# A post-norm decoder layer: the attention's weights loaded and split in smaller pieces

## The chip, the cores and the metric

The kernel runs on one core of one Trainium2 chip. The metric is the device time of one execution in microseconds (us). TensorE (PE) does the matrix products, ScalarE (ACT), VectorE (DVE) and GpSimd (POOL) the elementwise work, SyncE (SP) issues most of the transfers. ACT issues some transfers too. Each engine runs its own instructions strictly in the order written and meets the others by semaphores.

## The reference, cut to what matters

```python
# x: (8, 256, 256) f32; ctx: (8, 120, 256); Wq, Wk, Wv: (256, 1024); Wo: (1024, 256)
x = layernorm(x + attn(x, Wq, Wk, Wv, Wo, bo))     # 16 heads of 64, causal
x = layernorm(x + xattn(x, ctx, ...))              # 3 rounds of slot attention with a GRU
x = layernorm(x + ffn(x, gate, shared MLP, 8 experts, the best 2 per token))

def attn(x, Wq, Wk, Wv, Wo, bo):
    q, k, v = (x @ W, as 16 heads of 64) for Wq, Wk, Wv
    p = softmax(q k^T / 8 + causal mask)
    return (p v, heads joined) @ Wo + bo
```

## The kernel before, in words

The program has three stages, one for each line of the reference, with a barrier of all engines between the attention and the rest. The change touches the attention stage only.

**Two halves of a number.** A product of f32 numbers is done as three products of f16 numbers (`split_matmuls`, line 31): each operand is kept as a high part and a low part. A weight's high part is `wst * 64` rounded to f16, made by ACT (`weight_high`, line 607). Its low part is what the rounding left over, made by DVE from the same f32 weight and the high part (`weight_low`, line 683). `wst0` to `wst3` hold the f32 weights Wq, Wk, Wv, Wo, as 128 partitions of 2048 numbers each. `wqkv0`/`wqkv1` and `wo0`/`wo1` hold the high and low parts. DVE's instruction for a weight starts only when ACT's for that weight is done.

**Start.** SP issues the first tile pair of x (line 421), Wq, Wv, the other 12 tiles of x and then the ten transfers of the cross attention (line 171). ACT issues Wk, the second tile pair of x, Wo and the bias bo (lines 433 to 439). PE turns the two tile pairs of x with eight transposes (line 483). ACT casts each pair to its high part (line 600) and DVE makes its low part (line 675). ACT then makes the high parts of Wq, Wk and Wv in that order, and DVE their low parts.

**Steps.** After this start the engines run a loop over j from -2 to 66, one step for each of the 64 items. An item is one batch entry with one pair of heads, so item n uses the 128 columns `(n % 8) * 128` of Wq and Wk; `project_v` does two items at once and uses 256 columns of Wv. What each engine does in step j is written out by hand:

- PE: transposes of the probabilities of item j-1 (`turn_prob`, line 494), scores of item j+1 (line 521), values of item j-1 (`weigh_values`, line 531), the projection of q and k of item j+2 (line 31), in odd steps that of v for items j+1 and j+2, in even steps from 4 on a quarter of the output projection with Wo (`output_projection`).
- ACT: half of the turned probabilities (line 632), the heads' high part (line 639), exponentials of one head of item j+1 (line 617), q and k of item j+2 out of PSUM (lines 624, 625), exponentials of the other head.
- DVE: the other half of the turned probabilities (line 709), reciprocals (line 702), masks of item j+1 (line 695), the heads' low part (line 715), in even steps the values out of PSUM (line 721).
- POOL: the division of the probabilities (line 447) and, in steps 1, 9, 17 and so on, the addition of the bias to x (`add_bias`).

At the end of step 1 ACT makes the high part of the whole of Wo and DVE its low part. `output_projection` needs these from step 4 on. `turn_prob` reads probabilities, `weigh_values` needs both halves of the turned probabilities, of which ACT makes one (`probs_turned`, line 632) and DVE the other (line 709).

Of the kernel before, what the change touches and what calls it, by code (L numbers as in the profile page):

```python
# [11 lines left out]
ALU = mybir.AluOpType  # L12
# [3 lines left out]
P = 128  # L16
# [18 lines left out]
def decoder_layer(nc, a, out):  # L35
# [21 lines left out]
    with top:  # L57
# [55 lines left out]
        ident_cut = sem("ident_cut")  # L113
# [140 lines left out]
        def prep_vector(n):  # L254
            bank = ps[:, 6, :]
            VE.wait_ge(xw_mm, n + 1)
            if n < TURNS:
# [4 lines left out]
                if k == 0:  # L262
                    if s == 0:
                        VE.wait_ge(w_lo, 4)
# [34 lines left out]
        def context_squares(b):  # L299
            if b == 0:  # L300
                SC.wait_ge(xw_in, 16 * NLOAD)
                SC.wait_ge(w_lo, 4)
# [51 lines left out]
        with ExitStack() as c:  # L354
# [12 lines left out]
            rstd = sb(c, "rstd", [P, 2])  # L367

# [3 lines left out]
            w_hi, w_lo, bo_added = sem("w_hi"), sem("w_lo"), sem("bo_added")  # L372
# [17 lines left out]
            WQ, WK, WV, WO = range(4)  # L390

# [25 lines left out]
            def attention_sync():  # L417
# [4 lines left out]
                SY.dma_start(into[WQ], wv["q"]).then_inc(w_in[WQ], 16)  # L422
                SY.dma_start(into[WV], wv["v"]).then_inc(w_in[WV], 16)
# [7 lines left out]
            def attention_loads():  # L431
                xv = a["x"].rearrange("b (t p) d -> p (b t) d", p=P)
                SC.dma_start(wst[WK][:, :].rearrange("p (c n) -> p c n", c=DC),
                             a["L0_attn_Wk"].rearrange("(c p) n -> p c n", p=P)).then_inc(w_in[WK], 16)
                SC.dma_start(xs[:, 2:4, :], xv[:, 2:4, :]).then_inc(x_in[1], 16)
                SC.dma_start(wst[WO][:, :].rearrange("p (s n) -> p s n", s=PAIRS),
                             a["L0_attn_Wo"].rearrange("(s p) n -> p s n", p=P)).then_inc(w_in[WO], 16)
                bo_row = a["L0_attn_bo"].rearrange("(o d) -> o d", o=1)
                SC.dma_start(bo[:, :], bo_row.broadcast_to((P, D))).then_inc(bo_in, 16)
# [33 lines left out]
            def attention_tensor():  # L473
# [24 lines left out]
                def project_qk(n):  # L498
# [36 lines left out]
                def project_v(n):  # L535
# [4 lines left out]
                    else:  # L540
                        PE.wait_ge(v_out, n // 2)
                    for t in range(S // P):
# [5 lines left out]
                def output_projection(b, slot):  # L548
                    PE.wait_ge(o_lo, b * PAIRS + slot + 2)
                    PE.wait_ge(o_hi, b * PAIRS + slot + 2)  # L550
                    if b == 0:
                        PE.wait_ge(w_lo, 4)
                        PE.wait_ge(x_hi, 1)
                        PE.wait_ge(x_lo, 1)
                    elif slot == 0:
                        PE.wait_ge(y_added, b)
# [39 lines left out]
            def attention_scalar():  # L596
# [45 lines left out]
                inputs_high(0)  # L642
                inputs_high(1)
# [1579 lines left out]
```

## Time and profile before

| what | us |
|---|---|
| median of 3 runs | 979.01 |
| lowest and highest of them | 975.36, 981.52 |
| the profiled execution, its own time | 979.85 |
| its span, first to last instruction | 978.6 |
| PE busy in the span | 889.2 (91%) |
| DVE, ACT, POOL busy | 613.6, 554.1, 342.0 |
| mean granted clock of PE | 0.973 |

The profile is one execution. Times count from the start of the span. A row of the timeline gives start, length, engine, line and operation, and in brackets how long the engine sat idle ahead of it and which engine's result ended the idle time. A row with "x3" joins three instructions.

### The profile page before, as it was taken

The page shows a single profiled execution, that of the slowest core. Times are in us where ns is not written, and L with a number is a line of the kernel's source. Part 1 is how long each engine was busy: PE and PEld are TensorE (multiplying, and loading weights), DVE is VectorE, ACT ScalarE, POOL GpSimd, SP SyncE. Part 2 cuts the span into 40 slices and gives each one's busy share as a digit, 9 for nine tenths or more (in the row PEclk, how much of TensorE's full clock was granted, in tenths as well). Part 3 has the DMA queues.
Part 4 walks back from the last instruction along what each step waited for, and adds up shares of the span by engine and source line. Part 5 has one row for each costly group of instructions (what it writes and reads, how often), then busy time and mean ns, then how long its engine had stood idle before and what let it go on. Part 6 is the DMA issues. An engine that isn't in the chain of part 4 may idle for free.

```text
span 978.6 us, 23292 instructions
## 1 busy us (share of the span) xinstructions
PE 889.2 (91%) x8118; PEld 679.6 (69%) x8118; DVE 613.6 (63%) x1634; ACT 554.1 (57%) x1333; POOL 342.0 (35%) x456
## 2 busy tenths in 40 slices
PE   3899999999999998999999997798969999999980
PEld 2678878787777886666666665565647887888860
DVE  3456566655555554557776766799736666666653
ACT  3667756565555665556555653687725554555543
POOL 1333333332323432324433332347822233223233
PEclk9999999999999999999999999899979999999995
DMA  9900000000000000400100000347752322333326
GB/s 329 274 16 1 2 2 2 1 2 1 2 1 2 2 2 1 51 1 22 44 23 1 2 1 1 131 150 257 250 163 62 54 47 45 51 50 46 48 24 183
DMA packets 61117, 57.44 MB, mean 59 GB/s; under 512 B 19727, under 2 KB 56783, under 8 KB 60879
## 3 DMA queue, kind: packets, MB, share of 16 engines
q1 hardware_dynamic: 51039, 43.07, 15.3%
q0 software_dynamic: 7152, 9.34, 5.9%
q10 hardware_dynamic: 2816, 3.54, 1.0%
q8 instruction: 71, 1.16, 0.5%
q14 instruction: 39, 0.32, 0.1%
HBM read 37.13 MB, written 18.82 MB: 57 GB/s over the span
## 4 chain that ended last, share of the span: by engine, by line
PE 30%; POOL 10%; issue 8%; DVE 8%; ACT 3%; DMA 2%; DVEq 0%; POOLq 0%; ACTq 0%
PE ps L1960 11%; PE ps L1968 7%; PE ps L31 6%; POOL rows_x L1644 5%; PE ps L1969 3%; POOL dl L1347 2%; POOL sqs L1334 1%; DMA back_y<-slots,dst 1%; PE ps L337 1%; PE ps L1951 1%; POOL an L1351 1%; DVE t L1453 1%; DVE dl L1465 1%; DVE xs_row L865 1%; ACT hn L1263 1%
## 5 line engine op out<-in xcount | busy, mean ns | idle before, releaser
L1960 PE MATMUL ps<-slots,e 128*128 128x128 f16 x1872 | 191.0, 221 | 4.6 <-DVE slots L2092 2.3
L447 POOL TENSOR_SCALAR prob<-prob,rden 128x128 f32<-128x128 f32 (+1 forms) x256 | 104.0, 425 | 230.4 <-DVE rden L702 230.2
L1960 PEld LDWEIGHTS ps<-slots,e 128*128 x1872 | 154.1, 99 | 37.8 <-issue 6.2
L1928 POOL DMA_INDIRECT back_y<-slots,dst x39 | 67.5, 1730 | 173.6 <-ACT slots L2044 163.3
L1968 PE MATMUL ps<-e,sw 128*128 x312 | 117.9, 380 | 1.3 <-DVE sw L2082 1.3
L617 ACT ACTIVATE prob<-prob,nmx 128x128 f32<-128x128 f32 (+1 forms) x256 | 114.1, 452 | 4.3 <-DVE nmx L695 4.3
L2031 ACT ACTIVATE slots<-slots 128x512 f32<-128x512 f32 x78 | 49.1, 630 | 101.4 <-DVE slots L2077 101.4
L31 PE MATMUL ps<-s,whh 128*128 128x512 f16 x432 | 105.0, 378 | 0.0
L31 PE MATMUL ps<-xT,wqkv 128*128 128x256 f16 x768 | 98.4, 279 | 5.6 <-DVE wqkv L683 5.6
L31 PEld LDWEIGHTS ps<-xT,wqkv 128*128 128x128 f16 x768 | 71.2, 100 | 26.6 <-issue 16.9
L695 DVE CUSTOM_DVE_ANT_0 prob<-ps,mask 128x128 f32<-128x128 f32 (+1 forms) x256 | 80.4, 352 | 13.2 <-PE ps L521 13.2
L709 DVE COPY pT<-ps 128x384 f32<-128x384 f32 x64 | 35.6, 557 | 82.7 <-PE ps L494 81.5
L1969 PE MATMUL ps<-e,sw 128*128 x312 | 85.0, 273 | 0.0
L2077 DVE SCALAR_TENSOR_TENSOR slots<-ps,b1e 128x512 f32<-128x512 f32 x78 | 53.3, 687 | 36.5 <-PE ps L1960 36.1
L2082 DVE TENSOR_TENSOR sw<-slots,sw 128x1024 f16<-128x1024 f32 x39 | 47.8, 1225 | 39.9 <-ACT sw L2037 39.9
L639 ACT CAST oT<-ps 128x256 f16<-128x256 f32 x64 | 23.8, 373 | 84.7 <-PE ps L531 84.7
L31 PEld LDWEIGHTS ps<-s,whh 128*128 128x128 f16 x432 | 42.2, 101 | 35.6 <-issue 0.2
L531 PE MATMUL ps<-pT,v 128*64 128x128 f32 x768 | 56.7, 283 | 9.6 <-DVE pT L709 8.9
L531 PEld LDWEIGHTS ps<-pT,v 128*64 128x64 f32 x768 | 41.1, 137 | 31.9 <-DVE pT L709 30.5
L521 PE MATMUL ps<-qk 64*128 64x128 f32 (+1 forms) x512 | 60.0, 353 | 1.1 <-ACT qk L625 1.0
L31 PE MATMUL ps<-an,wqkv 120*128 120x256 f16 x432 | 59.1, 272 | 0.0
L1347 POOL TENSOR_TENSOR dl<-slots,nn 128x512 f32<-128x512 f32 x24 | 33.1, 1378 | 72.2 <-ACT nn L1271 72.2
(241 smaller groups left out, 1855.0 us busy)
## 6 DMA issues: line engine op xcount, KB each, us to landing
e<-in_L_ffn_ew SPq DMA_DIRECT2D x18, 512.0 KB
piece<-in_L_ffn_ew SPq DMA_DIRECT2D x12, 512.0 KB
rows_x<-zrow SPq DMA_DIRECT2D x1, 5031.0 KB, 19.0
xg<-rows_x SPq DMA_DIRECT2D x39, 128.0 KB, 2.5
piece<-in_L_ffn_sh_w SPq DMA_DIRECT2D x4, 512.0 KB
back_y<-xT SPq DMA_DIRECT2D x4, 512.0 KB, 3.9
out<-xs_row SPq DMA_DIRECT2D x8, 256.0 KB, 2.1
xs_row<-in_x SPq DMA_DIRECT2D x1, 1536.0 KB, 17.9
```

The lines of the kernel that those rows point to most:

```text
L31: mm = pe.matmul(out, w, x, start=first and n == 0, stop=last and n == len(products) - 1, **kw)
L447: PO.tensor_scalar(prob[m % 3][:, h, r], prob[m % 3][:, h, r], rden[m % 2][:, h, t:t + 1], 1.0, ALU.mult, ALU.mult).then_inc(normed, 1)
L521: mm = PE.matmul(ps[:, 2 + h, query_tile(t)], qk[m % 2][r, 0, t * P:t * P + P], qk[m % 2][r, 1, 0:(t + 1) * P], start=True, stop=True)
L531: mm = PE.matmul(ps[r, 4 + t, 384:512], v_sb[m // 2 % 2][:, key, m % 2, r], pT[:, h, at:at + P], start=key == 0, stop=key == t, skip_group ...
L617: SC.activation(p, p, ACT.Exp, bias=nmx[u][:, h, t:t + 1], scale=-1.0, accum_out=den[u][:, h, t:t + 1]).then_inc(exped, 1)
L695: VE.tensor_tensor_reduce(prob[m % 3][:, h, r], ps[:, 2 + h, r], mask[:, r], -1.0, HIGHEST, ALU.add, ALU.min, nmx[m % 2][:, h, t:t + 1]).t ...
L1347: PO.tensor_tensor(dl[:, :], slots[:, n % NG, ch, :], nn[:, :], ALU.subtract).then_inc(dl_out, 1)
L1928: PO.indirect_dma_start(back_y, bass.IndirectOffsetOnAxis(ap=dst[:, i:i + 1], axis=0), yo[i % 2], None, compute_op=ALU.add).then_inc(rows_ ...
L1960: yield PE.matmul(ps[:, 2 * u + q, (k % 4) * P:(k % 4) * P + P], w[ch][h], xgT[u][j][:, ch, :], start=n == 0, stop=n == 3 * DC - 1)
L1968: yield PE.matmul(ps[:, 4 + u, :], he[u][0][:, k, :], w, start=k == 0, stop=False, skip_group_check=True)
L1969: yield PE.matmul(ps[:, 4 + u, 0:D], he[u][1][:, k, :], w[:, 0:D], start=False, stop=k == IC - 1, skip_group_check=True)
L2077: VE.scalar_tensor_tensor(z, ps[:, 2 * u + q, :].rearrange("p (k t) -> p k t", k=4), 1 / WS, bias, ALU.mult, ALU.add).then_inc(U_bias, 1)
```

## The change

1. Wq, Wk and Wv are loaded by halves of their columns. The first halves (columns 0 to 511, items 0 to 3) come first: Wq's and Wv's on SP behind the first pair of x, Wk's on ACT's queue ahead of x's second pair. The three second halves follow on SP and share one semaphore, `w_rest`, which counts 48 when all three have landed.
2. Wo and the bias bo move from ACT's queue to SP's, behind those halves and ahead of the 12 tiles of x.
3. The weights are split in ten pieces (`CUTS`): six halves, then four quarters of Wo, each 128 x 512. The first three pieces are made at the start, the first two of them between the two pairs of x. The second halves are made at the ends of steps -2, -1, 0 on ACT and -1, 0, 1 on DVE, the quarters of Wo at the ends of steps 2, 3, 5 and 7 on both. PE waits for each piece ahead of the first matmul that reads it.
4. ACT runs one exponential on a 128 x 1 operand right behind its two DMA issues, so that its table load (`ACT_TABLE_LOAD`) stands there and not ahead of the first cast.
5. A semaphore nobody waits for, `ident_cut`, is gone.

```diff
+            FIRST_COLS = INNER // 2
+            CUTS = ((WQ, 0), (WK, 0), (WV, 0), (WQ, 1), (WK, 1), (WV, 1), (WO, 0), (WO, 1), (WO, 2), (WO, 3))
+            HIGH_AT = {-2: (3,), -1: (4,), 0: (5,), 2: (6,), 3: (7,), 5: (8,), 7: (9,)}
+            LOW_AT = {-1: (3,), 0: (4,), 1: (5,), 2: (6,), 3: (7,), 5: (8,), 7: (9,)}
+
+            def weight_part(t, n, h):
+
+                if n == WO:
+                    return t[:, 2 * h:2 * h + 2, :]
+                return t[:, :, h * FIRST_COLS:(h + 1) * FIRST_COLS]
...
-                SY.dma_start(into[WQ], wv["q"]).then_inc(w_in[WQ], 16)
-                SY.dma_start(into[WV], wv["v"]).then_inc(w_in[WV], 16)
+                SY.dma_start(into[WQ][:, :, 0:FIRST_COLS], wv["q"][:, :, 0:FIRST_COLS]).then_inc(w_in[WQ], 16)
+                SY.dma_start(into[WV][:, :, 0:FIRST_COLS], wv["v"][:, :, 0:FIRST_COLS]).then_inc(w_in[WV], 16)
+                for n, k in ((WQ, "q"), (WK, "k"), (WV, "v")):
+                    SY.dma_start(into[n][:, :, FIRST_COLS:INNER], wv[k][:, :, FIRST_COLS:INNER]).then_inc(w_rest, 16)
+                SY.dma_start(wst[WO][:, :].rearrange("p (s n) -> p s n", s=PAIRS),
+                             a["L0_attn_Wo"].rearrange("(s p) n -> p s n", p=P)).then_inc(w_in[WO], 16)
+                bo_row = a["L0_attn_bo"].rearrange("(o d) -> o d", o=1)
+                SY.dma_start(bo[:, :], bo_row.broadcast_to((P, D))).then_inc(bo_in, 16)
                 SY.dma_start(xs[:, 4:NT, :], xv[:, 4:NT, :]).then_inc(x_in[2], 16)
...
+                SC.dma_start(into[WK][:, :, 0:FIRST_COLS], wv["k"][:, :, 0:FIRST_COLS]).then_inc(w_in[WK], 16)
                 SC.dma_start(xs[:, 2:4, :], xv[:, 2:4, :]).then_inc(x_in[1], 16)
...
+                SC.wait_ge(const_fill, 4)
+                SC.activation(warm[:, :], powh[:, 0:1], ACT.Exp)
...
+                        if n == PAIRS // 2:
+                            PE.wait_ge(w_lo, k + 4)
...
                     if b == 0:
-                        PE.wait_ge(w_lo, 4)
+                        PE.wait_ge(w_lo, 7 + slot // 2)
+                    if b == 0 and slot == 0:
                         PE.wait_ge(x_hi, 1)
                         PE.wait_ge(x_lo, 1)
...
-                def weight_high(n):
-                    SC.wait_ge(w_in[n], 16)
+                def weight_high(i):
+                    n, h = CUTS[i]
+                    if n == WO or h == 0:
+                        SC.wait_ge(w_in[n], 16)
+                    else:
+                        SC.wait_ge(w_rest, 48)
...
-                    SC.mul(hi, src, WS).then_inc(w_hi, 1)
+                    SC.mul(weight_part(hi, n, h), weight_part(src, n, h), WS).then_inc(w_hi, 1)
...
                 inputs_high(0)
+                weight_high(0)
+                weight_high(1)
                 inputs_high(1)
-                for n in (WQ, WK, WV):
-                    weight_high(n)
+                weight_high(2)
...
-                    if j == 1:
-                        weight_high(WO)
+                    for i in HIGH_AT.get(j, ()):
+                        weight_high(i)
```

DVE's `weight_low` is cut in the same way and stands in the same places, by `LOW_AT`.

SP's queue at the start, before (Wq and Wv whole, then x's 12 tiles and the first transfer of the cross attention):

```order
L421 DMA xs_row<-in_x 128x2x256
L422 DMA wst0<-in_L0_attn_Wq 128x2x1024
L423 DMA wst2<-in_L0_attn_Wv 128x2x1024
L424 DMA xs_row<-in_x 128x12x256
L171 DMA sw<-in_L0_xattn_Wk 128x2x256
```

and of the change:

```order
L433 DMA xs_row<-in_x 128x2x256
L434 DMA wst0<-in_L0_attn_Wq 128x2x512
L435 DMA wst2<-in_L0_attn_Wv 128x2x512
L437 DMA wst0<-in_L0_attn_Wq 128x2x512
L437 DMA wst1<-in_L0_attn_Wk 128x2x512
L437 DMA wst2<-in_L0_attn_Wv 128x2x512
L438 DMA wst3<-in_L0_attn_Wo 128x8x256
L441 DMA bo<-in_L0_attn_bo 128x256
L442 DMA xs_row<-in_x 128x12x256
L170 DMA sw<-in_L0_xattn_Wk 128x2x256
```

Five halves instead of two whole weights stand here now (the sixth, Wk's first half, is on ACT's queue), then Wo and the bias, and the 12 tiles of x are ninth instead of fourth.

ACT's queue from its first instruction, before (`xT` is the high part of turned x, `wqkv0` the high part of a weight):

```order
L433 DMA wst1<-in_L0_attn_Wk 128x2x1024
L435 DMA xs_row<-in_x 128x2x256
L436 DMA wst3<-in_L0_attn_Wo 128x8x256
L439 DMA bo<-in_L0_attn_bo 128x256
L600 ACT_TABLE_LOAD
L600 CAST xT<-ps 128x2x256 x2
L607 ACTIVATE wqkv0<-wst0 128x2x1024
L607 ACTIVATE wqkv0<-wst1 128x2x1024
L607 ACTIVATE wqkv0<-wst2 128x2x1024
```

and of the change:

```order
L453 DMA wst1<-in_L0_attn_Wk 128x2x512
L454 DMA xs_row<-in_x 128x2x256
L456 ACT_TABLE_LOAD
L456 ACTIVATE warm<-powh 128x1
L622 CAST xT<-ps 128x2x256
L633 ACTIVATE wqkv0<-wst0 128x2x512
L633 ACTIVATE wqkv0<-wst1 128x2x512
L622 CAST xT<-ps 128x2x256
L633 ACTIVATE wqkv0<-wst2 128x2x512
L650 ACTIVATE qk0<-ps 128x256
L651 ACTIVATE qk0<-ps 128x256
L633 ACTIVATE wqkv0<-wst0 128x2x512
```

Two DMA issues left the head, the table load went from behind four issues to behind two, the first two pieces of weights went ahead of the second cast of x, and the second half of Wq stands behind the first q and k (`qk0`).

DVE's instructions of step 1, from its second masks back (`oT1` is the heads' low part, `wo1` that of Wo), before:

```order
L695 ISA nmx0 128x1
L715 TENSOR_TENSOR oT1<-ps,oT0 128x256
L695 ISA prob2,nmx0<-ps,mask 128x128
L695 ISA nmx0 128x1
L695 ISA prob2,nmx0<-ps,mask 128x256
L695 ISA nmx0 128x1
L683 SCALAR_TENSOR_TENSOR wo1<-wst3,wo0 128x2048
L709 COPY pT<-ps 128x384
```

and of the change first the end of step 0:

```order
L724 ISA nmx1 128x1
L750 TENSOR_SCALAR v0<-ps 128x512
L711 SCALAR_TENSOR_TENSOR wqkv1<-wst1,wqkv0 128x2x512
L738 COPY pT<-ps 128x384
L731 RECIPROCAL rden1<-den1 128x4
```

A half of Wk now stands between the values (`v0`) and the copy of the turned probabilities (`pT`) of item 0. The end of step 1 on DVE, of the change:

```order
L724 ISA prob2,nmx0<-ps,mask 128x256
L724 ISA nmx0 128x1
L711 SCALAR_TENSOR_TENSOR wqkv1<-wst2,wqkv0 128x2x512
L738 COPY pT<-ps 128x384
L731 RECIPROCAL rden0<-den0 128x4
```

A half of Wv stands where the whole of Wo stood. Wo's quarters stand at this place in steps 2, 3, 5 and 7.

## Rows read from the trace of the kernel before

**Rows 1.** Busy time by stretch (us; PE, PEld, DVE, ACT, POOL, clock, DMA share, GB/s)

```profile
0.00:50.00 50.00, 29.86 (x222) 21.66 (x224) 21.57 (x60) 25.04 (x66) 10.20 (x33) 0.97 1.01 301
60.00:320.00 260.00, 254.87 (x2425) 204.31 (x2425) 153.88 (x629) 156.77 (x577) 88.48 (x200) 1.00 0.01 2
```

**Rows 2.** DMA, first 50 us: GB/s in 40 slices; issues with us to landing

```profile
GB/s 0 14 244 395 415 399 433 397 397 378 357 360 347 349 352 356 348 347 351 344 351 280 185 198 185 47 224 325 336 337 300 245 287 310 336 334 325 274 294 272
...
wst<-in_L_attn_Wk ACTq DMA_DIRECT2D x1, 1024.0 KB, 6.1
wst<-in_L_attn_Wq SPq DMA_DIRECT2D x1, 1024.0 KB, 8.4
...
bo<-in_L_attn_bo ACTq DMA_DIRECT2D x1, 128.0 KB, 16.1
```

**Rows 3.** Timeline, 0 to 30 us, the start and the first steps

```profile
2.67 4.25 ACTq L439 DMA_DIRECT2D bo<-in_L_attn_bo  x1
...
6.96 1.28 ACT L600 ACT_TABLE_LOAD   x1 [6.96 <-issue]
...
10.57 1.11 PE L483 MATMUL ps<-ident,xs_row 128*128 128x128 f32 x4 [3.70 <-DMA xs_row<-in_x]
11.73 0.59 ACT L600 CAST xT<-ps 128x512 f16<-128x512 f32 x1 [2.89 <-PE ps L483]
12.21 5.51 ACT L607 ACTIVATE wqkv<-wst 128x2048 f16<-128x2048 f32 x3
...
12.35 0.69 DVE L675 TENSOR_TENSOR xT<-ps,xT 128x512 f16<-128x512 f32 x1 [2.79 <-ACT xT L600]
...
14.15 6.70 DVE L683 SCALAR_TENSOR_TENSOR wqkv<-wst,wqkv 128x2048 f16<-128x2048 f32 x3 [1.12 <-ACT wqkv L607]
...
16.59 1.44 PE L31 MATMUL ps<-xT,wqkv 128*128 128x256 f16 x6 [4.90 <-DVE wqkv L683]
...
18.71 1.46 PE L31 MATMUL ps<-xT,wqkv 128*128 128x256 f16 x6 [0.68 <-DVE wqkv L683]
...
20.92 1.65 PE L521 MATMUL ps<-qk 64*128 64x128 f32 x8 [0.75 <-ACT qk L625]
...
22.50 2.74 PE L31 MATMUL ps<-xT,wqkv 128*128 128x256 f16 x12
...
23.41 0.40 ACT L617 ACTIVATE prob<-prob,nmx 128x128 f32<-128x128 f32 x1 [2.55 <-DVE nmx L695]
...
25.03 1.74 PE L31 MATMUL ps<-wqkv,xT 128*128 128x256 f16 x12
...
26.83 0.18 DVE L702 RECIPROCAL rden<-den 128x4 f32<-128x4 f32 x1 [2.90 <-ACT prob L617]
...
27.57 1.48 PE L31 MATMUL ps<-xT,wqkv 128*128 128x256 f16 x12
...
28.36 0.40 ACT L617 ACTIVATE prob<-prob,nmx 128x128 f32<-128x128 f32 x1 [1.56 <-DVE nmx L695]
```

**Rows 4.** Timeline, 30 to 62 us: end of step 1, and one later step

```profile
31.17 0.88 PE L531 MATMUL ps<-pT,v 128*64 128x128 f32 x12 [0.31 <-ACT pT L632]
...
34.92 1.90 ACT L607 ACTIVATE wo<-wst 128x2048 f16<-128x2048 f32 x1
...
36.85 2.29 DVE L683 SCALAR_TENSOR_TENSOR wo<-wst,wo 128x2048 f16<-128x2048 f32 x1 [3.38 <-ACT wo L607]
...
39.67 1.55 PE L531 MATMUL ps<-pT,v 128*64 128x128 f32 x12 [3.38 <-DVE pT L709]
...
41.15 2.20 PE L31 MATMUL ps<-xT,wqkv 128*128 128x256 f16 x12
...
49.62 0.48 ACT L632 COPY pT<-ps 128x384 f32<-128x384 f32 x1 [0.44 <-PE ps L494]
49.62 0.56 DVE L709 COPY pT<-ps 128x384 f32<-128x384 f32 x1 [1.99 <-PE ps L494]
```

**Rows 5.** Busy time and granted clock of one stretch behind the stall

```profile
40.00:42.00 2.00, 2.00 (x17) 1.42 (x14) 0.56 (x3) 0.74 (x4) 1.42 (x4) 0.50 1.07 280
```

More of the change, by code:

```diff
@@ L301, in context_squares @@
                 SC.wait_ge(xw_in, 16 * NLOAD)
-                SC.wait_ge(w_lo, 4)
+                SC.wait_ge(w_lo, 10)
             else:
@@ L367, in decoder_layer @@
             rstd = sb(c, "rstd", [P, 2])
+            warm = sb(c, "warm", [P, 1])
             bo_in = sem("bo_in")
@@ L432, in attention_loads @@
                 xv = a["x"].rearrange("b (t p) d -> p (b t) d", p=P)
-                SC.dma_start(wst[WK][:, :].rearrange("p (c n) -> p c n", c=DC),
-                             a["L0_attn_Wk"].rearrange("(c p) n -> p c n", p=P)).then_inc(w_in[WK], 16)
+                wv = {k: a[f"L0_attn_W{k}"].rearrange("(c p) n -> p c n", p=P) for k in "qkv"}
+                into = [w[:, :].rearrange("p (c n) -> p c n", c=DC) for w in wst]
+                SC.dma_start(into[WK][:, :, 0:FIRST_COLS], wv["k"][:, :, 0:FIRST_COLS]).then_inc(w_in[WK], 16)
                 SC.dma_start(xs[:, 2:4, :], xv[:, 2:4, :]).then_inc(x_in[1], 16)
[L436 to L439, printed above, removed]
+                SC.wait_ge(const_fill, 4)
+                SC.activation(warm[:, :], powh[:, 0:1], ACT.Exp)
             def attention_pool():
@@ L541, in project_v @@
                         PE.wait_ge(v_out, n // 2)
+                    if n == PAIRS // 2:
+                        PE.wait_ge(w_lo, 6)
                     for t in range(S // P):
@@ L551, in output_projection @@
                     if b == 0:
-                        PE.wait_ge(w_lo, 4)
+                        PE.wait_ge(w_lo, 7 + slot // 2)
+                    if b == 0 and slot == 0:
                         PE.wait_ge(x_hi, 1)
                         PE.wait_ge(x_lo, 1)
-                    elif slot == 0:
+                    elif b >= 1 and slot == 0:
                         PE.wait_ge(y_added, b)
@@ L677, in inputs_low, with weight_low @@
                                      batch_xT(0, b), ALU.subtract).then_inc(x_lo, 1)
-                def weight_low(n):
-                    VE.wait_ge(w_hi, n + 1)
+                def weight_low(i):
+                    n, h = CUTS[i]
+                    VE.wait_ge(w_hi, i + 1)
                     hi, lo = ((w[:, :, n, :] for w in wqkv) if n < 3 else (w[:, :, :] for w in wo))
                     src = wst[n][:, :].rearrange("p (c n) -> p c n", c=DC if n < 3 else PAIRS)
-                    VE.scalar_tensor_tensor(lo, src, WS, hi, ALU.mult, ALU.subtract).then_inc(w_lo, 1)
+                    VE.scalar_tensor_tensor(weight_part(lo, n, h), weight_part(src, n, h), WS, weight_part(hi, n, h),
+                                            ALU.mult, ALU.subtract).then_inc(w_lo, 1)
                 def masks(m, h):
@@ L751, in attention_vector @@
                 inputs_low(0)
+                weight_low(0)
+                weight_low(1)
                 inputs_low(1)
-                for n in (WQ, WK, WV):
-                    weight_low(n)
+                weight_low(2)
                 VE.wait_ge(const_cut, 3)
@@ L775, in attention_vector @@
                         first_norm(batch_ending(j - 2))
-                    if j == 1:
-                        weight_low(WO)
+                    for i in LOW_AT.get(j, ()):
+                        weight_low(i)
                     if j == 9:
```

7 lines of the change are left out of this document (3 added, 4 removed).

## The prediction

> **What bounds the kernel now.** I first read busy time by stretch. From 60 to 320 us, inside the attention's loop, PE is busy 254.87 of 260 us, but in the first 50 us only 29.86 [rows 1]. So in the loop PE sets the pace, and whatever delays PE once moves the whole rest of the program; near the start PE waits. The change only touches those first 100 us, so I read the transfers there [rows 2], then the timeline of the start [rows 3] and of the end of step 1 [rows 4]. The reader is to see two holes. First, PE's projection of q and k for item 0 starts at 16.59 and ends at 18.71 + 1.46 = 20.17, although x's second pair has been turned by 10.57 + 1.11 = 11.68 [rows 3]. What stands between is ACT's three weights (12.21, 5.51 long) and DVE's (14.15, 6.70 long), a chain in which PE waits 4.90 us. Second, at 39.67 PE has waited 3.38 us for DVE's copy of turned probabilities; DVE was held by Wo, whose ACT half (34.92, 1.90) and DVE half (36.85, 2.29) stand one behind the other [rows 4].
>
> **Durations of the pieces.** A weight of 2048 columns takes ACT 1.90 [rows 4], or 1.8 where three follow each other (5.51 / 3); an ACT cast of 512 takes 0.59 [rows 3]. DVE takes 2.29 for 2048 [rows 4] and 0.69 for 512 [rows 3]. On straight lines between these, less the 0.08 to 0.1 by which neighbours overlap, a half (1024) takes 0.95 on ACT and 1.15 on DVE, a quarter of Wo (512) 0.50 and 0.61. Together they are within 0.2 us of the whole, so splitting costs little in itself.
>
> **The start.** Before, x's second pair landed at about 10.5 (PE's wait for it ends at 10.57) and Wq at 1.61 + 8.4 = 10.0 [rows 2, 3]. By then four transfers were in: Wk, Wq and two pairs of x, 2.5 MB. Of the change the same four are 1.5 MB. At the roughly 400 GB/s of that stretch [rows 2] this is 2.6 us less: I take 7.6 for Wq's first half and 7.9 for x's second pair. The ends: 6.9, if Wq's half gets ahead of x, and 10.0, if the landing doesn't move. ACT is ready in time: its table load stood at 6.96 only because its queue was still issuing the bias (2.67, 4.25 long) [rows 3]; now it stands at about 2.5. That by itself brings nothing, since before it too ended ahead of x's second pair.
>
> From there: ACT makes Wq's half from 7.6 to 8.55 and Wk's to 9.5. DVE makes them from 8.65 to 9.8 and to 10.95. PE projects q from 9.9 to 11.35 and k to 12.8, in 1.45 each as before. Before it was 20.17: **a gain of 7.4 us**. x's second pair (turned at 9.05) and Wv's first half are made behind these and are needed at 17. The bias's only reader is POOL's addition in step 1; it landed at 2.67 + 16.1 = 18.8 and now comes behind 3.75 MB on SP's queue, at about 16, for a step 1 that begins at about 22. Nobody needs x's other 12 tiles before step 5, nor the cross attention's ten transfers before step 8, so moving them back in SP's queue costs nothing; with that cover gone each us of lateness would cost one.
>
> **The second halves.** PE needs them at item 4, in step 2. ACT's half of Wq lies ahead of the first exponentials, where ACT had sat idle 2.55 us, DVE's behind the first masks, ahead of 2.90 idle us; ACT's half of Wk goes into 1.56 idle us [rows 3]. These cost nothing. DVE's half of Wk and ACT's half of Wv stand ahead of the copies of the turned probabilities of item 0, for which PE already waited 0.31 at 31.17 [rows 4]. The two run side by side: **a loss of 1.0**. It can be 0 (if those copies had room) to 2.1 (if one followed the other). DVE's half of Wv, in step 1, has its high part ready before DVE gets there and fits into the idle time where it stood before.
>
> **The hole at 36 to 39.67** goes: **a gain of 3.4**. What is late next there is nothing: DVE's copy comes right behind PE's transposes, and PE goes on. Behind the hole the granted clock was 0.50, so 1.2 GHz, from 40 to 42 [rows 5], and the product of values took 1.55 where its neighbour took 0.88, the projection 2.20 where its neighbour took 1.48 [rows 3, 4]: 0.67 + 0.72, **a gain of 1.4**, since no hole of such length is left.
>
> **Wo's quarters.** Each is a pair on two engines in one step, DVE waiting for ACT, with the copy of the turned probabilities behind. In step 2 PE has only one projection and no cover: ACT's 0.50, DVE's 0.61 and DVE's copy of 0.50 take the place of ACT's copy of 0.47, **a loss of 1.15**. In an odd step PE has v's projection too. There ACT is done with its exponentials 0.44 ahead of its copy at 49.62, at 49.18, and DVE has sat idle 1.99 [rows 4]. With a quarter DVE's copy ends at 49.18 + 0.50 + 0.61 + 0.50 = 50.8, instead of 50.2: 0.6, of which PE's own scores hide some 0.15. That is **0.45 each in steps 3 and 7** and, as PE turns x in step 5, **0.2 there**. For the four steps 2.25; bounds are 0 and the full 4 x 1.11 = 4.4.
>
> **The sum.** 7.4 - 1.0 + 3.4 + 1.4 - 1.15 - 1.1 = 8.95 us less. Against the profiled execution (979.85, span 978.6) this gives 970.9, against the median of 979.01 it gives 970.1. I take 970.5. Nothing behind the attention changes, and since PE is busy 98% of the loop [rows 1] the gain isn't absorbed there.
>
> **The clock at the start.** The slow durations there show PE at half its rate though the rows have no fall of the granted clock: the projection of 22.50 took 2.74 and that of 27.57 1.48; the one at 25.03, 1.74 long, holds the rise [rows 3]. So the rise came 8.5 to 9 us behind the first projection (16.59). I let it keep that distance. The Trainium skill (TensorE: Matmul & The Clock Gate, "Part 1: The HAM clock gate") says that the monitor runs free and isn't reset by the kernel, so that the rise does not keep a distance to the first matmul. By the one the sum stays, by the other it moves either way; this has its place among the rivals.
>
> **The rivals.**
> - *The clock rises earlier.* PE's work is denser now: 2.9 us of projection at a stretch, then the scores 0.8 us later, where before there were holes of 0.68 and 0.75 inside it. If the rise comes during the scores, they save 0.7 (1.65 against 0.93, the eight scores matmuls when fast), the projection 1.26 and v's 0.27, in all 2.0 as ACT becomes the limit in between: 968.5. For it: the denser start. Against it: before, the stretch from 18.71 to 22.50, four fifths busy, did not suffice either. Chance 0.18.
> - *The halves land no earlier.* If the time to 10 us is latency, not bytes, or halves move more slowly than whole rows, Wq's half comes at 10.0. Then q and k end at 15.2, a gain of 5.0 instead of 7.4: 973. For it: Wk on a queue of its own took 6.1 us for 1 MB [rows 2], over twice what its bytes take at 400 GB/s. Against it: the rate is at 400 GB/s from 3.75 us on, so the transfers are bound by bytes. Chance 0.15.
> - *The pieces are hidden better.* If the quarters and the step 1 halves cost 1.5 instead of 3.25: 968.8. Chance 0.12.
> - *Slower: the second halves come late.* All three share one semaphore, ACT waits for it in step -2, and behind this wait on ACT stand all exponentials. I expect them at 12 to 14; ACT's next work, the exponentials, comes at about 16, so the wait costs from about 15 on, 1 us for 1 us. It turns the gain into a loss from a landing at about 24 on; at 27 the time would be 979.85 - 8.95 + 12 = 982.9, and over 1% slower from 33 on. For it: one queue now carries them all, and the bias's issue on ACT's queue took 4.25 us behind 2.25 MB [rows 3]. Against it: they stand fourth to sixth, ahead of Wo, and x, Wk and Wq, 2.5 MB, were in by 10.5. Chance 0.03.
>
> **How the numbers follow.** Forecast 0.52, at 970.5 with a range of its own of 969 to 972. One per cent (969.2 to 988.8) is about what a measurement of this kernel can tell from no change, as three runs lie 0.6% apart. Faster by over 1%: most of the first and third rival (0.23) and a third of the forecast (0.17), 0.40. Slower by over 1%: no more than 0.03 with a margin for the rest. Within 1%: 0.57. The range from 966.5 to 974.5 holds the clock's and the landing's cases and the spread of the runs.
>
> **What would show it.** In the profile of the changed kernel: the table load at about 2.5; the first two weight pieces on ACT ending at about 9.5 and on DVE at 11; the end of the first q and k projection near 12.8; no wait of PE over 2 us between it and 100 us, and no granted clock below 1 there; PE waits of 1.0 to 1.7 us for the copies of turned probabilities in steps 1 and 2 and of about 0.4 in 3 and 7. It would be wrong if the first projection still ended behind 15, if ACT waited for the second halves with masks ready, or if the copies' waits added up to over 5 us.

## The result, and the profile after

| | before | changed kernel |
|---|---|---|
| median | 978.55 (5 runs, 975.36 to 981.52) | 970.24 (5 runs, 969.05 to 971.05) |
| the profiled execution, its time and its span | 979.85, 978.6 | 969.05, 967.8 |

The ratio is 0.9917, with a 95% interval of 0.9891 to 0.9942: 8.1 us faster, somewhere between 5.7 and 10.7. The forecast was 970.5, against a median of 970.24.

The total says little about the working, so the profile after is read by the steps of the sum. The timeline of the changed kernel's start (columns as in [rows 3]):

```profile
2.17 1.28 ACT L456 ACT_TABLE_LOAD   x1 [2.17 <-issue]
...
8.28 2.01 ACT L633 ACTIVATE wqkv<-wst 128x1024 f16<-128x1024 f32 x2 [1.35 <-DMA wst<-in_L_attn_Wq]
...
8.96 1.12 PE L500 MATMUL ps<-ident,xs_row 128*128 128x128 f32 x4 [2.66 <-DMA xs_row<-in_x]
9.37 2.36 DVE L711 SCALAR_TENSOR_TENSOR wqkv<-wst,wqkv 128x1024 f16<-128x1024 f32 x2 [1.72 <-ACT wqkv L633]
...
10.74 2.71 PE L31 MATMUL ps<-xT,wqkv 128*128 128x256 f16 x12 [0.67 <-DVE wqkv L711]
...
14.21 0.93 PE L540 MATMUL ps<-qk 64*128 64x128 f32 x8 [0.75 <-ACT qk L651]
...
15.06 1.48 PE L31 MATMUL ps<-xT,wqkv 128*128 128x256 f16 x12
...
20.48 2.09 DVE L711 SCALAR_TENSOR_TENSOR wqkv<-wst,wqkv 128x1024 f16<-128x1024 f32 x1
...
21.73 1.05 ACT L633 ACTIVATE wqkv<-wst 128x1024 f16<-128x1024 f32 x1
...
23.20 0.88 PE L550 MATMUL ps<-pT,v 128*64 128x128 f32 x12 [1.08 <-ACT pT L658]
```

Against [rows 3]: the table load stands at 2.17 and not at 6.96. Wq's first half lands at 8.28, where ACT's wait for it ends. The first projection runs from 10.74 to 13.45, where it had ended at 20.17. The scores of item 0 take 0.93 where they took 1.65, and the next projection 1.48 where it took 2.74, so PE's rate had risen by 14.2 already. The halves that stand ahead of the copies of step 1 (20.48 on DVE, 21.73 on ACT) make PE wait 1.08 us at 23.20, where it had waited 0.31 [rows 4].

The timeline of the changed kernel from 31 to 42 us, Wo's first two quarters:

```profile
31.99 0.62 ACT L633 ACTIVATE wo<-wst 128x512 f16<-128x512 f32 x1
...
32.65 0.69 DVE L711 SCALAR_TENSOR_TENSOR wo<-wst,wo 128x512 f16<-128x512 f32 x1 [1.50 <-ACT wo L633]
33.25 0.55 DVE L738 COPY pT<-ps 128x384 f32<-128x384 f32 x1
...
33.86 1.29 PE L550 MATMUL ps<-pT,v 128*64 128x128 f32 x12 [1.65 <-DVE pT L738]
...
35.08 2.69 PE L31 MATMUL ps<-xT,wqkv 128*128 128x256 f16 x12
...
41.10 0.88 PE L550 MATMUL ps<-pT,v 128*64 128x128 f32 x12 [0.51 <-DVE pT L738]
```

The hole of 3.38 us at 39.67 [rows 4] is gone. In its place PE waits 1.65 us at 33.86: ACT's quarter (31.99), DVE's (32.65) and DVE's copy (33.25) follow each other. In step 3 the same three make it wait 0.51 us. And the product of values at 33.86 takes 1.29, the projection behind it 2.69 instead of 1.49. The granted clock there, by stretch:

```profile
33.00:34.00 1.00, 0.14 (x2) 0.14 (x4) 1.00 (x6) 0.00 (x0) 0.01 (x1) 1.00 0.31 31
...
35.00:36.00 1.00, 1.00 (x7) 0.68 (x6) 0.41 (x2) 0.82 (x4) 0.62 (x2) 0.50 0.15 12
...
38.00:39.00 1.00, 1.00 (x11) 0.91 (x10) 0.00 (x0) 1.00 (x5) 0.00 (x0) 1.00 1.04 349
```

It fell to 0.50 (1.2 GHz) behind a hole half as long as the one that [rows 5] showed it behind.

Busy time by stretch (columns as in [rows 1]) and the landings (as in [rows 2]) of the changed kernel:

```profile
0.00:50.00 50.00, 37.12 (x314) 28.14 (x315) 25.73 (x86) 30.82 (x95) 13.52 (x41) 0.97 0.96 284
60.00:320.00 260.00, 254.51 (x2418) 204.41 (x2416) 153.10 (x625) 157.60 (x581) 87.97 (x197) 1.00 0.01 2
```

```profile
wst<-in_L_attn_Wq SPq DMA_DIRECT2D x2, 512.0 KB, 7.6
...
wst<-in_L_attn_Wk ACTq DMA_DIRECT2D x1, 512.0 KB, 5.3
wst<-in_L_attn_Wk SPq DMA_DIRECT2D x1, 512.0 KB, 9.3
...
bo<-in_L_attn_bo SPq DMA_DIRECT2D x1, 128.0 KB, 12.1
```

In the first 50 us PE is busy 37.12 us instead of 29.86; in the loop its share is as before. Wk's second half, issued at 3.25, landed at 12.6, where I had expected the second halves at 12 to 14, and the bias, issued at 5.21, at 17.3, 3 us ahead of its reader at 20.30.

To compare kernels I take the start of one PE instruction group in each profile, the product of values of item 12 (step 13). All pieces of weights are made by then, and from there to item 55 the kernels keep their distance: in the profiles of before and after the two groups of item 12 start at 96.62 and 88.52, those of item 55 at 339.83 and 331.72, 8.1 us apart both times. What comes behind item 12 is the same code in every kernel, but took between 877.7 and 885.4 us in the profiles. That spread is as large as the whole effect, which is why a row in the first 100 us tells more here than a median. The granted clock goes with it: behind item 12 the profile of e12 spent 40 us at 0.50 (1.2 GHz) and took 877.9 us, that of e4 spent 55 us there and took 885.4. Over the fourteen profiles the two go together, though not exactly, and which falls of the clock come in one execution differs for the same kernel (45 us in e1, 43 in the first profile of the change).

### The profile page after: what moved, and what is told of

Its sections match the earlier page's. It is cut to its first block, busy times and chain, and to the rows that moved or that the text cites. A ratio compares the mean times of both kernels' runs of the same rounds, so it can differ in the third digit from the quotient of the medians.

```text
span 967.8 us, 23307 instructions
## 1 busy us (share of the span) xinstructions
PE 887.7 (92%) x8118; PEld 677.8 (70%) x8118; DVE 614.4 (63%) x1640; ACT 554.6 (57%) x1340; POOL 339.9 (35%) x456
## 4 chain that ended last, share of the span: by engine, by line
PE 30%; POOL 9%; issue 8%; DVE 8%; ACT 2%; DMA 2%; SPq 1%; DVEq 0%; POOLq 0%; ACTq 0%
PE ps L1990 10%; PE ps L1998 7%; PE ps L31 6%; POOL rows_x L1674 4%; PE ps L1999 3%; POOL dl L1377 2%; POOL sqs L1364 1%; DMA back_y<-slots,dst 1%; PE ps L336 1%; POOL an L1381 1%; PE ps L1981 1%; DVE t L1483 1%; DVE dl L1495 1%; DVE xs_row L895 1%; ACT hn L1293 1%
```

## The experiments

All times in us. "Item 12" is the start named above. "Rise" says whether PE was at full rate for the scores of item 0 (early, they take 0.93) or not (late, 1.65 or 1.66); "fall" whether the granted clock fell later in the first 60 us. The ratio is the one on record for the run, against the kernel before on the same chip; the quotient of the two medians can differ from it by 0.002 (e9: 966.89 against 981.11 is 0.9855).

| run | median | ratio (95%) | end of first projection | item 12 | rise | fall |
|---|---|---|---|---|---|---|
| before | 978.55 | | 20.17 | 96.62 | late | yes |
| after | 970.24 | 0.9917 (0.9891 to 0.9942) | 13.45 | 88.52 | early | yes |
| e1 the change again | 972.11 | 0.9934 (0.9912 to 0.9956) | 13.17 | 86.61 | early | no |
| e2 start only | 969.98 | 0.9921 (0.9892 to 0.9949) | 13.37 | 89.04 | late | no |
| e3 quarters only | 978.00 | 0.9992 (0.9971 to 1.0012) | 20.28 | 95.35 | late | no |
| e4 whole loads | 975.25 | 0.9946 (0.9924 to 0.9968) | 15.17 | 90.61 | late | no |
| e5 table early | 979.26 | 1.0004 (0.9984 to 1.0024) | 19.99 | 96.60 | late | yes |
| e6 high early | 969.11 | 0.9884 (0.9856 to 0.9911) | 13.35 | 84.17 | early | no |
| e7 odd steps only | 969.83 | 0.9885 (0.9851 to 0.9920) | 13.43 | 88.35 | late | no |
| e8 no early exponential | 973.15 (1 run) | | 13.05 | 86.50 | early | no |
| e9 = e6 again | 966.89 | 0.9873 (0.9845 to 0.9901) | 13.01 | 83.82 | early | no |
| e10 ACT's pieces mid-step | 968.76 | 0.9877 (0.9846 to 0.9908) | 13.44 | 85.64 | late | no |
| e11 spare transposes | 968.47 | 0.9879 (0.9851 to 0.9907) | 13.37 | 86.04 | late | no |
| e12 spare matmuls | 965.49 | 0.9876 (0.9844 to 0.9907) | 13.15 | 83.97 | early | no |

**e1, the changed kernel again.** No edit.

> The changed kernel, unchanged, for a second profile. Theory: the start, the waits for copies of turned probabilities (1.1 us in step 1, 1.65 in step 2, about 0.5 in 3, 5 and 7) and the gain up to item 12 without the clock repeat within 0.3 us; where PE's rate rises at the start and whether it falls behind step 2 is not tied to the program, so the product of values of item 12 starts between 88 and 91 (88.52 in the first profile). Rival: the early rise comes from the denser start and the fall behind step 2 from the 1.65 us wait, then both stand in the same places again and item 12 starts at 88.5 within 0.3. Median 970.2, within 1.5.

The waits came back to within 0.01 us in the timeline of PE:

```profile
33.57 0.88 PE L550 MATMUL ps<-pT,v 128*64 128x128 f32 x12 [1.65 <-DVE pT L738]
34.38 1.48 PE L31 MATMUL ps<-xT,wqkv 128*128 128x256 f16 x12
...
39.19 0.88 PE L550 MATMUL ps<-pT,v 128*64 128x128 f32 x12 [0.51 <-DVE pT L738]
```

The same 1.65 us, but 0.88 and 1.48 behind it: this time the clock did not fall. From item 2 to item 3 it took 39.19 - 33.57 = 5.62 us, and 41.10 - 33.86 = 7.24 in the first profile, so the fall cost 1.6, and this wait does not always bring one. The rise was early both times. Item 12 came at 86.6, before the range I gave (88 to 91), which had been worked out from the first profile without taking off its fall. The median, 972.11, lies 0.4 above the range given for it (970.2 within 1.5).

**e2, the start alone.** Wo is split whole in step 1, as before.

```diff
-            CUTS = (..., (WO, 0), (WO, 1), (WO, 2), (WO, 3))
-            LOW_AT = {-1: (3,), 0: (4,), 1: (5,), 2: (6,), 3: (7,), 5: (8,), 7: (9,)}
+            CUTS = (..., (WO, 0))
+            LOW_AT = {-1: (3,), 0: (4,), 1: (5, 6)}
```

> The change without Wo's quarters: Wo is split whole at the end of step 1 as before. Theory: the first projection ends at 13.4 as in the changed kernel, the wait of PE over 3 us for the copy in step 2 is back and with it a granted clock of 0.50 behind it; the gain over the kernel before is the start's 6.7, plus up to 2.0 if the clock rises early, minus 1.0 for the halves in steps 0 and 1: 5.7 to 7.7, so about 972. Rival: the hole takes up what the start gains (Wo or DVE were late for another reason, such as a landing), then the gain is under 3: 976 or more.

PE's timeline:

```profile
14.12 1.66 PE L540 MATMUL ps<-qk 64*128 64x128 f32 x8 [0.75 <-ACT qk L651]
15.71 2.62 PE L31 MATMUL ps<-xT,wqkv 128*128 128x256 f16 x12
...
24.98 0.88 PE L550 MATMUL ps<-pT,v 128*64 128x128 f32 x12 [1.26 <-ACT pT L658]
...
33.48 0.88 PE L550 MATMUL ps<-pT,v 128*64 128x128 f32 x12 [3.39 <-DVE pT L738]
34.29 1.48 PE L31 MATMUL ps<-xT,wqkv 128*128 128x256 f16 x12
```

The hole is back at its old length, 3.39 us, so the start's gain isn't taken up by it. But behind the hole the product takes 0.88: the clock did not fall, against what I expected. From item 0 to item 12 this kernel takes 89.04 - 24.98 = 64.06 us, the changed kernel in e1 86.61 - 22.91 = 63.70. So once no clock falls, **Wo's quarters are worth 0.4 us**: they remove 3.4 and cost almost as much. The ratios say the same: 0.9921 without the quarters, 0.9917 and 0.9934 with them. Practically all of the measured gain is the start's.

**e3, the quarters alone,** in the kernel before.

```diff
-                    if j == 1:
-                        weight_low(WO)
+                    if j in (2, 3, 5, 7):
+                        weight_low(WO, (2, 3, 5, 7).index(j))
```

> The kernel before with only Wo's split in quarters in steps 2, 3, 5 and 7. Theory: 3.4 for the hole and 1.4 for the clock behind it are gained, 1.3 + 0.5 + 0.3 + 0.6 = 2.7 are lost in the four steps, and another 1.6 if the clock falls behind step 2's wait as it did in the changed kernel: a gain of 0.5 to 2.1, 977 to 978. Rival (prediction's own count, no fall): 2.5 or more, 976.

PE's timeline:

```profile
25.15 2.35 PE L31 MATMUL ps<-wqkv,xT 128*128 128x256 f16 x12
...
31.90 0.88 PE L531 MATMUL ps<-pT,v 128*64 128x128 f32 x12 [0.31 <-ACT pT L635]
...
42.57 0.88 PE L531 MATMUL ps<-pT,v 128*64 128x128 f32 x12 [1.66 <-DVE pT L714]
```

PE waits 1.66, 0.51, 0.67 and 0.52 us in the four steps, as the changed kernel did, and no clock fell. The median of 978.00 is at the upper end of what I expected, and the ratio's interval holds 1. Item 12 came 1.3 us sooner than before. But item 0 came 0.7 later (31.90 against 31.17), for the most part because PE's rate rose later: v's projection at 25.15 took 2.35 us, where it had taken 1.74 [rows 3]. From item 0 to item 12 it takes 95.35 - 31.90 = 63.45 us, where the kernel before took 96.62 - 31.17 = 65.45, of which its fall of the clock cost 1.4. So the quarters alone are worth 0.6 us, which agrees with the 0.4 of e2.

**e4, whole loads.** The change, with Wq, Wk and Wv loaded in one transfer each, on the same queues.

```diff
-                SY.dma_start(into[WQ][:, :, 0:FIRST_COLS], wv["q"][:, :, 0:FIRST_COLS]).then_inc(w_in[WQ], 16)
+                SY.dma_start(into[WQ], wv["q"]).then_inc(w_in[WQ], 16)
```

> The changed kernel with Wq, Wk and Wv each loaded whole in one transfer (splitting still by halves, queues and order as in the change). Theory: landings follow bytes, Wq whole lands at about 10 instead of 8.3, the first projection ends 1.7 later than 13.4, at 15.1, and this much is lost: 971.9. Rival: the gain of the start is from splitting in pieces alone and latency sets the landing: no loss, 970.2.

ACT's timeline:

```profile
9.99 2.00 ACT L628 ACTIVATE wqkv<-wst 128x1024 f16<-128x1024 f32 x2 [2.67 <-DMA wst<-in_L_attn_Wq]
11.90 0.57 ACT L620 CAST xT<-ps 128x512 f16<-128x512 f32 x1
...
15.20 0.38 ACT L645 ACTIVATE qk<-ps 128x256 f32<-128x256 f32 x1 [1.49 <-PE ps L31]
```

Wq lands at 9.99 instead of 8.28, and the first projection ends at 15.17 instead of 13.45. So of the 6.7 us at the start, 5.0 come from splitting in pieces (20.17 to 15.17) and 1.7 from loading in pieces. The median lies 3.1 above e1's and 3.3 above the 971.9 that I expected. The profile has a late rise of the clock and spent 55 us at 0.50 behind item 12, so this median isn't the landing's price alone, and what I read here is the row.

**e5, the table early,** with Wo and the bias on SP's queue, in the kernel before.

```diff
+                SC.wait_ge(const_fill, 4)
+                SC.activation(warm[:, :], powh[:, 0:1], ACT.Exp)
```

> The kernel before with only the move of Wo and the bias to SP's queue and ScalarE's early table load. Theory: the table load leaves 6.96 for 2.2, but the first projection waits for x's second pair, Wq and the three whole weights, so it still ends at 20 to 20.3: no change, 978.5 within 0.5. Rival: the table load was on the path, or Wo off ACT's queue lets x's second pair land sooner: a gain of 1 us or more, 977.5 or less.

The table load went to 2.15, x's second pair landed 0.17 us sooner (10.40 instead of 10.57), and the first projection ended at 19.99. No gain came of it. This profile too has a fall of the clock with the hole of 3.38 us: from item 0 to item 12 it took 96.60 - 30.39 = 66.21 us, where e2 with such a hole and no fall took 64.06, so this fall cost 2.2.

**e6, high parts early.** Each quarter's high part is made a step or two ahead of its low part, and the low parts stand in steps 3, 5, 7 and 9. As the low parts end later now, one more number is changed: ACT waits for six and not for all ten of them in step 8 (`SC.wait_ge(w_lo, 6)`). The later runs but e8 have this too.

```diff
-            HIGH_AT = {-2: (3,), -1: (4,), 0: (5,), 2: (6,), 3: (7,), 5: (8,), 7: (9,)}
-            LOW_AT = {-1: (3,), 0: (4,), 1: (5,), 2: (6,), 3: (7,), 5: (8,), 7: (9,)}
+            HIGH_AT = {-2: (3,), -1: (4,), 0: (5,), 1: (6,), 3: (7,), 5: (8,), 7: (9,)}
+            LOW_AT = {-1: (3,), 0: (4,), 1: (5,), 3: (6,), 5: (7,), 7: (8,), 9: (9,)}
```

> The changed kernel with the high parts of Wo's quarters at the ends of steps 1, 3, 5 and 7 and the low parts at the ends of steps 3, 5, 7 and 9, so that DVE never waits for ACT's piece of the same step. Theory: the wait of 1.65 us in step 2 and those of 0.5 to 0.7 in 3, 5 and 7 go (to under 0.3 each), no fall of the clock behind step 2: 2.7 of the changed kernel's losses and 1.6 of the fall are won, 966 to 967.5. Rival: the copies are late for ACT's part as well (its piece stands ahead of its own copy), then half of the waits stay: 968.5.

PE's timeline:

```profile
32.41 0.88 PE L550 MATMUL ps<-pT,v 128*64 128x128 f32 x12 [0.31 <-ACT pT L658]
...
48.59 0.88 PE L550 MATMUL ps<-pT,v 128*64 128x128 f32 x12 [0.54 <-DVE pT L738]
```

PE's waits in steps 3 and 7 are gone, that in step 2 is back to 0.31, that in step 5 is 0.54. From item 0 to item 12 it takes 84.17 - 23.09 = 61.08 us, 2.6 less than e1; e7 tells how much of this comes from the early high parts and how much from the other steps. The median came out 1.6 above the range given, and in e9 within it.

**e7, odd steps only.** Both parts of a quarter in steps 3, 5, 7 and 9, by both tables as in e6's `LOW_AT`.

> The changed kernel with Wo's quarters, both parts in the same step as in the change, at the ends of steps 3, 5, 7 and 9. Theory: step 2's 1.3 us becomes 0.5 in step 9, and the fall of the clock behind step 2 (1.6) goes with its wait: 968 to 969.5. Rival: the fall has nothing to do with step 2's wait; then only 0.8 is won, 969.5, and a granted clock of 0.50 stands somewhere in the first 60 us all the same.

PE waits 0.31 in step 2, then 0.51, 0.67, 0.51 and 0.78 us. From item 0 to item 12 it takes 63.20, 0.5 less than e1: moving the first quarter out of the step without cover helps by half a microsecond. e6 differs from this run only in where ACT makes the high parts, and takes 61.08: making them early is worth 2.1. So DVE's wait for ACT's piece inside one step was most of what the quarters cost. The median, 969.83, is 0.3 above the range given. No fall was seen; by e1 that is no evidence for either side.

**e8, without the early exponential,** in the changed kernel.

```diff
-                SC.wait_ge(const_fill, 4)
-                SC.activation(warm[:, :], powh[:, 0:1], ACT.Exp)
```

> The changed kernel without ScalarE's early exponential (and its wait on a semaphore). Theory: the table load was late in the kernel before because the bias's issue held ACT's queue to 6.92; with two issues left on it the load stands at about 2.2 by itself, and the first cast at 6.3, so the early exponential does nothing. Rival: the table load waits for what its cast waits for and comes at 6.3, the first cast at 7.6; ACT is then ready at 8.2, still ahead of Wq's half at 8.28, so the time is the same but the row moves.

The table load stands at 2.17 all the same, as the first engine instruction behind ACT's two transfers. What moved it was taking the bias and Wo off this queue. The exponential does nothing.

**e9, e6 again.**

> The kernel with the quarters' high parts a step or two ahead of their low parts, once more, to be compared with the next two on the same chip. Median 969.1 within 1; its waits of PE as before (1.1 or 1.25 in step 1, 0.3 in step 2, 0.5 in step 5), item 12's product of values at 84.2 with an early rise of the clock and at 86.2 with a late one.

966.89, 2.2 under e6's median and 1.2 below the range given, on a chip on which the kernel before had 981.11 instead of 979.02. The ratios, 0.9884 and 0.9873, agree.

**e10, ACT's pieces in the middle of a step,** between its copy of the probabilities and the cast of the heads.

```diff
+            MID_AT = {1: (5,), 2: (6,), 4: (7,), 6: (8,), 8: (9,)}
...
                         probs_turned(j - 1)
+                        for i in MID_AT.get(j, ()):
+                            weight_high(i)
                         heads_high(j - 1)
```

> As e9, but ACT makes its pieces in the middle of a step, where it waits about 1 us for the product of values (0.97 to 1.19 in every step), DVE's half of Wk goes to the end of step 1 and that of Wv to step 2. Theory: PE's wait of 1.1 us in step 1 falls to 0.3 or less and no other grows by more than 0.4: item 12 0.5 to 0.9 earlier than e9 with the same clock, 968.4. Rival: ACT's piece delays the heads' cast and everything behind it, item 12 is later than e9.

DVE's half of Wk moved to the end of step 1 and that of Wv to step 2. PE's wait in step 1 fell from 1.26 (e11, which has a late rise too) to 0.31, that in step 5 from 0.54 to 0.35, and that in step 2, where DVE's half of Wv now stands, grew from 0.31 to 0.59: 0.86 us less waiting. Item 12 came at 85.64, against 86.04 in e11, only 0.4 sooner, because PE's rate rose later in this profile (v's first projection took 1.77 us, in e11 1.47), so that the next scores began 0.46 later. By the waits the move is worth 0.9, which no profile with the same rise confirms. The medians can't tell it from e9's.

**e11, spare transposes.** e6 with twenty transposes of the identity while PE has nothing to do.

```diff
-                for b in range(X_EARLY):
-                    turn_inputs(b)
+                for b, spare in enumerate((11, 8, 1)):
+                    for _ in range(spare):
+                        PE.transpose(ps[:, 5, 0:P], ident[:, :], ident[:, :])
+                    if b < X_EARLY:
+                        turn_inputs(b)
```

> As e9, with twenty transposes of the identity more on PE (11 ahead of x's first pair, 8 between the pairs, 1 behind), whose results nobody reads. Theory: PE's rate rises when PE has been busy for some us, not at a fixed time; with work from 2 us on it is at full rate by the first projection, which takes 1.5 to 1.9 instead of 2.7 and ends 0.8 to 1.2 sooner, and the scores of item 0 take 0.93 in every profile: item 12 at 83 to 83.4, the median 1 to 2.5 us under e9's (e9's executions have an early and a late rise mixed). Rival: the rise at the start isn't set by what PE did; then the first projection takes 2.7 again and the median is e9's.

The timeline of PE:

```profile
1.90 2.61 PE L589 MATMUL ps<-ident 128*128 128x128 f32 x11 [1.90 <-POOL ident L118]
...
6.29 1.91 PE L589 MATMUL ps<-ident 128*128 128x128 f32 x8
...
10.66 2.71 PE L31 MATMUL ps<-xT,wqkv 128*128 128x256 f16 x12 [0.42 <-DVE wqkv L714]
14.12 1.66 PE L540 MATMUL ps<-qk 64*128 64x128 f32 x8 [0.75 <-ACT qk L654]
```

and its busy time by stretch (the second number after the window; columns as in [rows 1]):

```profile
2.00:5.00 3.00, 2.51 (x11) 2.11 (x11) 0.20 (x1) 1.49 (x2) 1.72 (x10) 1.00 0.80 226
5.00:8.00 3.00, 2.61 (x12) 2.42 (x12) 0.69 (x1) 0.59 (x1) 0.00 (x0) 1.00 1.04 375
```

PE was busy 2.51 of the 3 us from 2 to 5 and 2.61 of the next 3, and the first projection took 2.71 all the same, with the late rise behind it. The theory as I had put it, that any work of PE raises its rate, fell. The median is 1.6 above e9's, not 1 to 2.5 under it.

**e12, spare matmuls.** The same with 24 ordinary matmuls (13, 9 and 2) in place of the transposes.

```diff
-                        PE.transpose(ps[:, 5, 0:P], ident[:, :], ident[:, :])
+                        PE.matmul(ps[:, 5, 0:P], ident[:, :], ident[:, :], start=True, stop=True)
```

> As the run with twenty spare transposes, but with 24 ordinary matmuls of the identity by itself (13 ahead of x's first pair, 9 between the pairs, 2 behind). Theory after that run: a transpose doesn't count as work for the clock (the Trainium skill, TensorE: Matmul & The Clock Gate, says so of the transpose mode), an ordinary matmul does; then the first projection runs fast, 1.5 to 2.0 us instead of 2.3 to 2.7, the scores of item 0 take 0.93, and item 12 starts at 83 to 83.8. Rival: what PE did before the projection isn't what decides the rise; then the projection takes 2.3 us or more, and item 12 starts at 83.8 or at 86.1 as before.

The timeline of PE:

```profile
1.90 5.91 PE L589 MATMUL ps<-ident 128*128 128x128 f32 x26 [1.90 <-POOL ident L118]
7.61 0.68 PE L500 MATMUL ps<-ident,xs_row 128*128 128x128 f32 x4
...
10.14 0.60 PE L500 MATMUL ps<-ident,xs_row 128*128 128x128 f32 x4
...
11.27 0.82 PE L31 MATMUL ps<-xT,wqkv 128*128 128x256 f16 x6
12.32 0.83 PE L31 MATMUL ps<-xT,wqkv 128*128 128x256 f16 x6 [0.23 <-DVE wqkv L714]
13.89 0.93 PE L540 MATMUL ps<-qk 64*128 64x128 f32 x8 [0.75 <-ACT qk L654]
```

The two halves of the first projection take 0.82 and 0.83 instead of 1.44 and 1.46 [rows 3]: PE is at full rate for all of it. Even the four transposes of x, from 7.61 on, take 0.68 and 0.60, where they took 1.1; in no other profile did the rate rise before the first projection had begun. So work of PE ahead of it can raise the rate, and ordinary matmuls did. In e11 the rate rose only near the end of the projection at 15.71 (2.60 us), just as in e2 (2.62), which has no spare work: the transposes changed nothing. That a transpose doesn't count is what the Trainium skill says of transpose mode (TensorE: Matmul & The Clock Gate, "Part 4: PE-mode transpose"), and e11 beside e12 agrees. One rival is left: e12 kept PE busy without a break from 1.90 to 11.0, while e11 had holes of 0.88 and 0.70 us in that time, and each is one profile. A run with as many matmuls and e11's holes would tell. The gain at item 12 is small, since the first 13 matmuls (each is two in the records) took 5.91 us and held up x's turn to 7.61; item 12 missed the range I gave by 0.2. Against a late rise (e11) it is 2.1 sooner, against an early one (e9) no sooner.

e6, e7, e9, e10, e11 and e12 have ratios of 0.9873 to 0.9885, below the changed kernel's 0.9917 and 0.9934, though most of the intervals overlap. By ratio e7 can't be told from e6; by item 12 with the rise taken off it is 2.1 us behind. The version to keep is e6's, about 1.2% under the kernel before. e12 has the lowest median, 965.49, but its interval is e6's.

## Why the prediction was right or wrong, point by point

The forecast of 970.5 was met within 0.3 us. The parts are another matter. In the profiles of before and after item 0 came 31.17 - 23.20 = 7.97 us sooner, by 6.7 from the start and 2.0 from the early rise, less 0.8 for the second halves. From item 0 to item 12, where hole, quarters and clock were to bring 3.4 - 2.25 + 1.4 = 2.55, the changed kernel was only 65.45 - 65.32 = 0.13 us faster. Point by point:

- **The start: 7.4 forecast, 6.7 measured.** The mechanism was right: two pieces and not three whole weights ahead of the first projection. Wq's half landed 0.7 us later than taken (8.28, not 7.6), which the range of 6.9 to 10.0 held; ACT's half took 1.0 and DVE's 1.2, where I had 0.95 and 1.15. For the earlier landing I had taken 2.4 us, from 2.6 by bytes at 400 GB/s, and it was 1.7 (e4): this is the term of the start that was too large. The rival that halves land no earlier fell, but its figure for splitting alone, 5.0, is exactly what e4 shows.
- **The second halves: 1.0 forecast, 0.8 to 0.95 measured** (waits of 1.08 with an early and 1.26 with a late rise, against 0.31). The others, in idle time, cost nothing, as forecast. ACT never waited for the second halves' semaphore, so the rival that ends slower had nothing to stand on.
- **The hole: 3.4, as forecast.** e2 brings it back at 3.39.
- **Wo's quarters: 2.25 forecast, 2.7 measured** (1.34, 0.51, 0.32, 0.51). The term was undersized (1.15, 0.45, 0.2, 0.45): ACT's quarter takes 0.62 and DVE's 0.69, since in this chain of two engines the piece's full length counts, not its distance to the next on the same engine, which I had used. A further wait of 0.21 in step 10 stands in every profile that has both the changed start and the quarters, and neither in e2 nor in e3. The sum had no term for it, and its cause is open.
- **The clock behind the hole: 1.4 forecast, not shown to belong to the change. Here a step failed.** I wrote "a gain of 1.4, since no hole of such length is left". A hole of that length is neither needed nor enough: the fall came with 3.38 us in two profiles (before, e5) but not with 3.39 in e2, and it came behind 1.65 in the first profile of the change but not in the second, nor behind e3's, e4's and e8's waits of 1.65. The six profiles without a wait over 1.26 us there (e6, e7, e9 to e12) have none. So the term holds in some executions only; a fall cost 1.4 to 2.2 us where it came. Whether the changed kernel has it more seldom than the kernel before (one profile in three, after, e1 and e8, against two in two, before and e5) so few profiles can't tell.
- **The rise at the start. Here too a step failed.** "I let it keep that distance": it did not. With the changed start and no spare work on PE the rise came early in five profiles (after, e1, e6, e8, e9) and late in three (e2, e7, e10), with 2.0 us between, the price that I had worked out for the rival *the clock rises earlier* (0.18). With the start of before it was late three times in three (before, e3, e5), and with whole loads too (e4). So the rise does not keep its distance to the first projection, and a chance of about a half would have been right. That the denser start is what makes an early rise possible was the reason I gave; three profiles of the old start are too few to show it.

Without any clock effect the sum is 6.7 - 0.9 + 3.4 - 2.7 - 0.2 = 6.3. The rise adds 2.0 in five profiles of eight, so 1.2 on average, together 7.5, and perhaps some part of the fall. The forecast of 8.95 had 1.4 for the fall and nothing for the rise, and 1.2 too much in the rest. The errors nearly cancelled: that the median came within 0.3 us was luck. The two measured ratios say 8.1 and 6.5 us.

Also right: one per cent was the edge. The interval of the ratio doesn't reach 1, and the measured gain, 0.8%, is under 1%, though its interval goes to 1.1%.

## What to carry to other kernels

Where a weight is split by two engines, one behind the other, put the first engine's part a step ahead of the second's: that was worth 2.1 us here (e7 against e6), while cutting the same work in quarters and leaving the pair in one step gave back all but 0.4 of the hole it closed. Whether an early high part would do as well with Wo left whole wasn't tried. At a start, cut what stands before the first product to what that product needs: splitting by halves gave 5.0 us, loading by halves another 1.7. And compare small changes at a row that ends the changed part, not at the end of a program whose unchanged rest varies by as much as the effect.

## What the runs showed of the hardware that was not expected

- PE's rate at the start was raised by ordinary matmuls and not by transposes: with twenty spare f32 transposes ahead of it, the first projection took 2.71 us, with 24 spare f32 matmuls 1.65 (0.82 + 0.83). The matmuls also ran without the transposes' holes of 0.88 and 0.70 us, which was not tested apart.
- Holes of the same length, at nearly the same time, are followed by a granted clock of 0.50 in one execution and not in the next: 3.4 us in two of three profiles, 1.65 us in one of five. With no wait over 1.26 us there, none of six profiles had one.
- DVE's half of Wk in step 0 takes 2.09 us, while the same instruction takes 1.21 or 1.22 elsewhere. POOL's addition of the bias runs beside it, from 20.30 for 1.18 us:

```profile
20.30 1.18 POOL L471 TENSOR_TENSOR xs_row<-xs_row,bo 128x512 f32<-128x512 f32 x1
```

The two overlap for 1.00 us and DVE takes 0.87 longer. In the profiles with a late rise (e2, e4, e7, e11) they overlap for only 0.72 to 0.75 us, and DVE's half takes 1.80 to 1.82, so 0.58 to 0.60 longer. In e10, where the half stands a step later without that addition beside it, it takes 1.22. So while the addition ran, DVE's instruction made next to no progress. It cost nothing here, as ACT's copy was the later one (it ends at 23.15, DVE's at 23.04).
